# Padding the tiles that TensorE reads to different places modulo 128 bytes in a Mamba2 and Q4 feed-forward kernel

## The chip, the core and the metric

The kernel is one program on one core of a Trainium2 chip. The time is device microseconds from the start to the end of that core's execution. Lower is better. The host only lays data out before the launch.

## What is computed

The input `x` is `(2, 512, 512)`. It is layer-normalised, and two branches read the result: a Mamba2 mixer `s` and a feed-forward net `g` with 4-bit weights. The output is `x + s * silu(g)`.

```python
xn = _layernorm(x)
# mixer: 128 heads of 64, state size 128, 8 groups, chunks of 128 tokens
proj = xn @ in_proj_w.T                       # gate 8192 | x 8192, B 1024, C 1024 | dt 128
xBC  = silu(conv4(xBC) + conv_b)              # depthwise, 4 taps
y    = ssd(x, B, C, D, dt, dt_bias)           # chunked selective scan
yg   = y * silu(gate)
out  = (yg / rms over each group of 1024) * norm_w
s    = out @ out_proj_w.T                     # 8192 -> 512
# feed-forward: Q4_0 weights, hidden size 1376
h    = silu(xn @ W1.T) * (xn @ W3.T)
g    = h @ W2.T
result = x + s * silu(g)
```

## The kernel before

Everything in SBUF is float32. A matrix product with full precision is made of three passes: every operand is split into a high part (rounded to float32r, names ending in `_hi`) and a low part (the rest, `_lo`), and `split_mm` (lines 132 to 138) issues for each of four slices of the contraction, `KT = 4`, the three products high by high (L135), high by low (L136, L137). In `pe.matmul(dst, a, b)` the first operand `a` is the **stationary** one: 128x128, loaded by a weight load (LDWEIGHTS, rows of PEld). The second, `b`, is the **moving** one: it streams 512 columns through the array. The views print `bank<-moving,stationary`.

```python
    for i, (a_hi, a_lo, b_hi, b_lo) in enumerate(terms):
        pe.matmul(dst, a_hi, b_hi, start=(i == 0), stop=False)
        pe.matmul(dst, a_hi, b_lo, start=False, stop=False)
        mm = pe.matmul(dst, a_lo, b_hi, start=False, stop=(i == len(terms) - 1))
```

The mixer goes over 16 bodies (8 groups of heads by 2 sequences) with 8 steps each, 128 steps in all, written out without a loop, by `over_bodies`. The order on every engine is written out by hand, and the steps are software-pipelined: the projections of later steps stand between the scan's pieces of this one. One step of TensorE (`step` inside `@block.tensor`, line 696) is, for nearly all of them:

- `y_off`: 3 float32 matmuls (6 records) with `state` stationary and `c_t` moving, L543;
- `conv`: 12 matmuls 128x512 with `conv_hi`/`conv_lo` stationary, `xn_hi`/`xn_lo` moving, L135 to L137;
- `y_diag`: 8 float32 matmuls (16 records) with `xdt` stationary and `lm` moving, L585, then 3 (6 records) with `b_tok` stationary and `xw` moving, L543;
- `gate_mm`: 12 matmuls with `gate_hi`/`gate_lo` stationary, `xn` moving, L135 to L137;
- `out_mm`: 12 matmuls with the results `y_hi`/`y_lo` **stationary** and the weights `wout_hi`/`wout_lo` **moving**, L631 to L633;
- `extra` and `turn_x`: the B and C projections (12 matmuls each, once a body), and transposes of `xt` or `b_t`, moving `ident`, L693 and L654.

The weight load of each matmul is a record of its own and runs beside the matmul before it. After the mixer the feed-forward stage runs 528 matmuls of the same form (`up_hi`, `up_lo` stationary, `xn` moving) and 33 products of the down projection for each of 8 token tiles (`h` stationary, `w2` moving, L831; the last tile in two halves). The other engines round, split, mask, activate and combine beside this; ScalarE, VectorE and GpSimd wait for TensorE by semaphores and TensorE for them.

Tiles are allocated by `alloc` (line 165) as a stack: each starts where the last one ended, a size is taken up to whole 32 bytes per partition, and a closed scope gives its space to the next. The first tile starts at byte 16512 of each partition. `ctx` holds for the whole kernel, `main` for the mixer, `pre` for the setup, and the feed-forward tiles lie over `main`. All matrices have rows of 512 bytes or more, so that a tile's place modulo 128 is also the place of all its slices. `sh` with its 32 bytes puts everything from `xn_hi` to the end of `cw_all` at 32 modulo 128; `cw_all` (1600 bytes) moves what follows to 96.

Of the kernel before, what the change touches and what calls it, by code (L numbers as in the profile page):

```python
# [22 lines left out]
R32 = mybir.dt.float32r  # L23
I32 = mybir.dt.int32

P = 128
SEQS, SEQ, DIM = 2, 512, 512
KT = DIM // P
HEADS, HD = 128, 64
GROUPS, CHUNK = 8, 128  # L30
INTER = HEADS * HD
GCH = INTER // GROUPS
HALF = GCH // 2
GH = HEADS // GROUPS
NC = SEQ // CHUNK
TT = SEQS * SEQ // P
CONVS = GCH // P + 2
TILES = GCH // P
# [10 lines left out]
SH = 4  # L49
# [101 lines left out]
def build(nc, x, w_conv, w_gate, w_out, w_dt, conv_p, norm_p, head_p, consts, w1q, w1s, w3q, w3s,  # L151
# [9 lines left out]
    with ExitStack() as ctx:  # L161
# [3 lines left out]
        def alloc(stack, name, shape, dt=F32):  # L165
            return stack.enter_context(nc.sbuf_tensor(name, [P] + shape, dt))


        ident = alloc(ctx, "ident", [P])
        mask = alloc(ctx, "mask", [P])  # L170
        sh = alloc(ctx, "sh", [2, SH], I32)
        xn_hi = alloc(ctx, "xn_hi", [KT, SEQS * SEQ], R32)
        xn_lo = alloc(ctx, "xn_lo", [KT, SEQS * SEQ], R32)

        main = ExitStack()

        conv_hi = [alloc(main, f"conv_hi{i}", [KT, P], R32) for i in range(3)]
        conv_lo = [alloc(main, f"conv_lo{i}", [KT, P], R32) for i in range(3)]
        raw_x = alloc(main, "raw_x", [2, DIM])
        raw_b = alloc(main, "raw_b", [DIM])  # L180
        raw_g = alloc(main, "raw_g", [DIM])
        raw_o = alloc(main, "raw_o", [DIM])
        z = alloc(main, "z", [3, SEQ])
        b_t = alloc(main, "b_t", [SEQ])
        cw_all = alloc(main, "cw_all", [GROUPS, CONVS, 5])
        gate_hi = [alloc(main, f"gate_hi{h}", [KT, HALF], R32) for h in range(2)]
        gate_lo = [alloc(main, f"gate_lo{h}", [KT, HALF], R32) for h in range(2)]
        c_t = alloc(main, "c_t", [2, SEQ])
        nw_all = alloc(main, "nw_all", [GROUPS, TILES])
        dc_all = alloc(main, "dc_all", [GROUPS, TILES])  # L190
        xt = alloc(main, "xt", [4, SEQ])
        gm = alloc(main, "gm", [NC, CHUNK])
        b_tok = alloc(main, "b_tok", [NC, P])
        gate = alloc(main, "gate", [4, SEQ])
        lm = [alloc(main, f"lm{i}", [2 * NC, CHUNK]) for i in range(3)]
        hp = [alloc(main, f"hp{h}", [NQ, TILES, 2 * NC]) for h in range(2)]
        rstd = alloc(main, "rstd", [NC])
        rstd_sum = alloc(main, "rstd_sum", [NC])
        neg_half = alloc(main, "neg_half", [8])
        one = alloc(main, "one", [1])  # L200

        pre = ExitStack()


        x_in = alloc(pre, "x_in", [TT, DIM])
        stage = alloc(pre, "stage", [NQ, GROUPS, TILES, 2 * NC])
        wdt_raw = alloc(pre, "wdt_raw", [KT, P])
        wdt_hi = alloc(pre, "wdt_hi", [KT, P], R32)
# [1 line left out]
        ecs = alloc(pre, "ecs", [TT, CHUNK])  # L210
        soft = alloc(pre, "soft", [TT, CHUNK])
        wdt_lo = alloc(pre, "wdt_lo", [KT, P], R32)
        heads = alloc(pre, "heads", [3])
        d_row = alloc(pre, "d_row", [P])
        pick = alloc(pre, "pick", [2, P // 2])
# [6 lines left out]
        wout_hi, wout_lo = [], []  # L222
        for h in range(2):
            wout_hi.append(alloc(main, f"wout_hi{h}", [4, DIM], R32))
            wout_lo.append(alloc(main, f"wout_lo{h}", [4, DIM], R32))
            if h == 0:
                acc = alloc(main, "acc", [TT, DIM])
        sq = alloc(main, "sq", [SEQ])
        sq_sum = alloc(main, "sq_sum", [SEQ])
        y_hi = alloc(main, "y_hi", [2, SEQ], R32)  # L230
        y_lo = alloc(main, "y_lo", [2, SEQ], R32)
        yt = alloc(main, "yt", [2, SEQ])
        ec = [alloc(main, f"ec{i}", [(NC - 1) * CHUNK]) for i in range(2)]
# [1483 lines left out]
```

How the kernel before makes its waits and increments, by code:

```python
def wait(eng, sem, count):  # L84
    if isinstance(count, int) and count <= 0:
        return
    eng.wait_ge(sem, count)
# [253 lines left out]
        def token_steps(eng, b):  # L342
            eng.wait_ge(pa, (N_SOFT + N_EXPS) * b + N_SOFT)
            eng.wait_ge(pd, N_PD * b + 1)
            eng.tensor_tensor(qt[Q_DT][:, half[b], :], qt[Q_DT][:, half[b], :], ecs[:, half[b], :],
                              ALU.add).then_inc(dt_done, 1)
            eng.wait_ge(dt_done, 3 * b + 1)
            eng.tensor_scalar(qt[Q_DT][:, half[b], :], qt[Q_DT][:, half[b], :], DT_MIN, DT_MAX, ALU.max,
                              ALU.min).then_inc(dt_done, 1)
            eng.wait_ge(dt_done, 3 * b + 2)
            eng.tensor_scalar(qt[Q_CD][:, half[b], :], qt[Q_DT][:, half[b], :], heads[:, 2:3], None,
                              ALU.mult).then_inc(dt_done, 1)
# [10 lines left out]
        def wait_gate_piece(eng, group, pos):  # L364
            if group == 0 and pos < 4:
                eng.wait_ge(gate0_in[pos], 16)
            else:
                eng.wait_ge(rawg_in, 16 * (8 * group + pos - 3))
# [9 lines left out]
        def wait_hp(eng, body):  # L378
            if body.n == 0:
                eng.wait_ge(hp0_ev, NQ)
            else:
                eng.wait_ge(hp_in[body.seq], 16 * (body.group + body.seq))
# [1 line left out]
        def store_out(sp, t):  # L385
            sp.wait_ge(r2_done, t + 1)
            h = col_parts(t)[0]
            sp.dma_start(out_t[t][:, h], fh[:, t % 2, h]).then_inc(o_out[t % 2], 16)
```

## Time and profile before

| | before |
|---|---|
| median of 3 runs | 1791.61 us |
| lowest, highest | 1790.51, 1792.0 us |
| span of the profiled execution, first to last instruction | 1789.9 us |
| TensorE busy (PE) | 1775.3 us, 99% |
| weight loads (PEld) | 1462.1 us, 82% |
| VectorE (DVE) | 1427.3 us, 80% |
| GpSimd (POOL) | 1262.4 us, 71% |
| ScalarE (ACT) | 1228.8 us, 69% |

The profiled execution has no time of its own beside its span; the median of the runs is 1.7 us above this span, which is what lies before the first and behind the last instruction. Busy time of a group of matmuls is the union of its records. A record lasts longer than the distance to the next one's start, because matmuls are pipelined, so a group's count times its mean is more than its busy time. A mean duration of one is therefore read against another's, and the cost of a matmul is the distance between two starts in the timeline.

### The profile page before, as it was taken

Reading aid. Unit: us, or ns where it says so; the run is one execution under the profiler, and the core shown is the slowest. Engines: PE = TensorE matmul, PEld = TensorE weight load, DVE = VectorE, ACT = ScalarE, POOL = GpSimd, SP = SyncE. Lnnn points to the kernel's source line nnn. Section 1 sums busy time; section 2 is a strip of 40 time slices with the busy share of each in tenths; the row PEclk is TensorE's granted clock in tenths of the full one; section 3 lists DMA queues with packets and bytes.
Section 4 is the critical chain, followed back from the end, with each engine's and each line's share of the span. In section 5 each row is a group of like instructions: output and inputs, shape, how many; then the busy total and the mean of one; then the engine's idle time right before and its main releaser. Section 6 shows DMA issues by size and latency. Waiting matters only on the chain.

```text
span 1789.9 us, 30329 instructions
## 1 busy us (share of the span) xinstructions
PE 1775.3 (99%) x10357; PEld 1462.1 (82%) x10357; DVE 1427.3 (80%) x2196; ACT 1228.8 (69%) x2456; POOL 1262.4 (71%) x877
## 2 busy tenths in 40 slices
PE   8999999999999999999999999999999999999999
PEld 7788888888888888888888888888888888888877
DVE  7978878878788788788787887887887888878941
ACT  6986777777776777677866777677777677643320
POOL 5677787777777687677776786777776777676630
PEclk9999999999999999999999999999999999999999
DMA  5433333233333242333333342333333333235522
GB/s 200 160 123 101 99 130 107 93 121 107 117 107 110 96 134 94 102 110 116 119 104 95 118 122 96 115 98 117 115 96 111 107 123 101 77 108 162 151 78 94
DMA packets 122595, 202.84 MB, mean 113 GB/s; under 512 B 23056, under 2 KB 60560, under 8 KB 122192
## 3 DMA queue, kind: packets, MB, share of 16 engines
q1 hardware_dynamic: 120720, 197.32, 34.9%
q10 hardware_dynamic: 1728, 3.65, 0.5%
q8 instruction: 82, 1.34, 0.3%
q14 instruction: 65, 0.53, 0.1%
HBM read 193.57 MB, written 7.34 MB: 112 GB/s over the span
## 4 chain that ended last, share of the span: by engine, by line
PE 95%; DVE 3%; POOL 1%; issue 1%; DMA 1%; SPq 0%; ACT 0%; POOLq 0%; DVEq 0%; ACTq 0%
PE bank L137 16%; PE bank L135 16%; PE bank L136 16%; PE bank L543 11%; PE bank L585 7%; PE bank L631 7%; PE bank L633 6%; PE bank L632 6%; PE bank L831 3%; PE bank L693 3%; PE bank L674 1%; DVE z L1189 0%; PE bank L654 0%; DMA q_s<-w1s_dram 0%; DVE x_in L1341 0%
## 5 line engine op out<-in xcount | busy, mean ns | idle before, releaser
L1518 POOL TENSOR_TENSOR yt<-yt,ec 128x384 f32<-128x384 f32 x128 | 174.8, 1366 | 329.7 <-DVE ec L1253 329.7
L1189 DVE SCALAR_TENSOR_TENSOR z<-bank,cw_all,z 128x511 f32<-128x511 f32 (+2 forms) x477 | 356.3, 747 | 11.7 <-ACT z L944 0.5
L905 ACT ACTIVATE lm<-lm,hp 128x128 f32<-128x128 f32 x1024 | 313.2, 390 | 0.8
L1244 DVE TENSOR_TENSOR xdt<-bank,hp 128x512 f32<-128x512 f32 x128 | 88.3, 690 | 222.3 <-PE bank L693 221.0
L135 PE MATMUL bank<-xn_hi,conv_hi 128*128 128x512 f32 x640 | 261.7, 409 | 3.5 <-DVE z L1189 3.4
L1223 DVE SCALAR_TENSOR_TENSOR lm<-lm,gm 128x1024 f32<-128x1024 f32 x128 | 261.2, 2040 | 3.4 <-ACT lm L905 3.4
L137 PE MATMUL bank<-xn_hi,conv_lo 128*128 128x512 f32 x640 | 251.7, 393 | 0.0
L136 PE MATMUL bank<-xn_lo,conv_hi 128*128 128x512 f32 x640 | 250.5, 391 | 0.0
L1522 POOL TENSOR_TENSOR yt<-yt,gate 128x512 f32<-128x512 f32 x128 | 226.7, 1771 | 19.0 <-POOL yt L1518 0.9
L1527 POOL TENSOR_TENSOR conv_lo<-raw_x,conv_hi 128x512 fp32r<-128x512 f32 x124 | 218.4, 1762 | 9.9 <-ACT conv_hi L844 9.8
L944 ACT ACTIVATE z<-bank,cw_all 128x512 f32<-128x512 f32 x128 | 99.1, 774 | 166.5 <-PE bank L137 166.5
L135 PE MATMUL bank<-xn_hi,gate_hi 128*128 128x512 f32 x512 | 212.3, 415 | 0.0
L631 PE MATMUL bank<-wout_hi,y_hi 128*128 128x512 f32 x512 | 202.6, 396 | 0.0
L137 PE MATMUL bank<-xn_hi,gate_lo 128*128 128x512 f32 x512 | 202.0, 395 | 0.0
L136 PE MATMUL bank<-xn_lo,gate_hi 128*128 128x512 f32 x512 | 201.8, 394 | 0.0
L633 PE MATMUL bank<-wout_hi,y_lo 128*128 128x512 f32 x512 | 200.6, 392 | 0.0
L632 PE MATMUL bank<-wout_lo,y_hi 128*128 128x512 f32 x512 | 199.2, 389 | 0.0
L1210 DVE SCALAR_TENSOR_TENSOR lm<-hp,lm 128x1024 f32<-128x1024 f32 x128 | 194.5, 1520 | 0.0
L1504 POOL TENSOR_TENSOR y_lo<-yt,y_hi 128x512 fp32r<-128x512 f32 x128 | 182.3, 1424 | 3.0 <-ACT y_hi L976 3.0
L1554 POOL TENSOR_TENSOR sq_sum<-sq_sum,sq 128x512 f32<-128x512 f32 x111 | 145.1, 1307 | 21.2 <-ACT sq L984 21.2
L585 PEld LDWEIGHTS bank<-lm,xdt 128*64 128x64 f32 x2048 | 109.2, 136 | 45.9 <-issue 44.6
L137 PEld LDWEIGHTS bank<-xn_hi,conv_lo 128*128 128x128 f32 x640 | 120.4, 188 | 26.7
(145 smaller groups left out, 3950.9 us busy)
## 6 DMA issues: line engine op xcount, KB each, us to landing
lm<-cs_d SPq DMA_DIRECT2D x128, 512.0 KB, 4.0
raw_x<-w_conv_dram SPq DMA_DIRECT2D x128, 256.0 KB, 3.1
ec<-e_d SPq DMA_DIRECT2D x256, 96.0 KB, 3.6
raw_o<-w_out_dram SPq DMA_DIRECT2D x64, 256.0 KB, 2.7
raw_g<-w_gate_dram SPq DMA_DIRECT2D x61, 256.0 KB, 2.7
raw_b<-w_conv_dram SPq DMA_DIRECT2D x32, 256.0 KB, 3.4
q_raw<-w1q_dram SPq DMA_DIRECT2D x10, 256.0 KB, 3.8
q_s<-w1s_dram SPq DMA_DIRECT2D x10, 256.0 KB, 4.1
```

What stands on the lines that cost most here:

```text
L135: pe.matmul(dst, a_hi, b_hi, start=(i == 0), stop=False)
L136: pe.matmul(dst, a_hi, b_lo, start=False, stop=False)
L137: mm = pe.matmul(dst, a_lo, b_hi, start=False, stop=(i == len(terms) - 1))
L585: mm = pe.matmul(ps_y[HD * j:HD * j + HD, c * P:(c + 1) * P], xdt[:, c * P + HD * j:c * P + HD * j + HD], lm[n % 3][:, NC * j + c, :], sta ...
L631: pe.matmul(ps_o[c][:, :], y_hi[:, ko % 2, o], w[0], start=first, stop=False)
L632: pe.matmul(ps_o[c][:, :], y_hi[:, ko % 2, o], w[1], start=False, stop=False)
L633: mm = pe.matmul(ps_o[c][:, :], y_lo[:, ko % 2, o], w[0], start=False, stop=last)
L905: e = act.activation(lm[m % 3][:, u, :], lm[m % 3][:, u, :], ACT.Exp, bias=hp[bd.seq][:, Q_CS, k1, u:u + 1])
L1189: dve.scalar_tensor_tensor(dst[:, d:SEQ], src[:, 0:SEQ - d], cw_all[:, bd.group, pos, 3 - d:4 - d], dst[:, d:SEQ], ALU.mult, ALU.add).then ...
L1223: dve.scalar_tensor_tensor(lm_c, lm_c, 1.0, gm[:, :, :].rearrange("p c l -> p (c l)").unsqueeze(1) .broadcast_to((P, 2, SEQ)), ALU.mult, A ...
L1522: pool.tensor_tensor(yt[:, kp % 2, :], yt[:, kp % 2, :], gate[:, kp % 4, :], ALU.mult).then_inc(yg_done, 1)
L1527: pool.tensor_tensor(conv_lo[kx % 2][:, :, :], raw_x[:, kx % 2, :].rearrange("p (k j) -> p k j", k=KT), conv_hi[kx % 2][:, :, :].bitcast(F ...
```

## The change

The change adds small tiles that nobody reads or writes (`shift(name)`, 32 bytes; two of 160 bytes) and allocates the small tiles (`sh`, `rstd`, `rstd_sum`, `neg_half`, `one`, `nw_all`, `dc_all`, `cw_all`) first. No instruction is added, removed or moved on any engine: the programs of before and after differ in line numbers and in addresses alone.

```diff
+        sh = alloc(ctx, "sh", [2, SH], I32)
...
+        cw_all = alloc(ctx, "cw_all", [GROUPS, CONVS, 5])
+        alloc(ctx, "to_line", [40])
         ident = alloc(ctx, "ident", [P])
         mask = alloc(ctx, "mask", [P])
-        sh = alloc(ctx, "sh", [2, SH], I32)
         xn_hi = alloc(ctx, "xn_hi", [KT, SEQS * SEQ], R32)
...
-        conv_hi = [alloc(main, f"conv_hi{i}", [KT, P], R32) for i in range(3)]
-        conv_lo = [alloc(main, f"conv_lo{i}", [KT, P], R32) for i in range(3)]
+        def shift(name):
+            alloc(main, name, [8])
+
+        conv_hi, conv_lo = [], []
+        for i in range(3):
+            if i == 1:
+                shift("sh_ch")
+            conv_hi.append(alloc(main, f"conv_hi{i}", [KT, P], R32))
+        for i in range(3):
+            if i < 2:
+                shift(f"sh_cl{i}")
+            conv_lo.append(alloc(main, f"conv_lo{i}", [KT, P], R32))
...
-        gate_hi = [alloc(main, f"gate_hi{h}", [KT, HALF], R32) for h in range(2)]
-        gate_lo = [alloc(main, f"gate_lo{h}", [KT, HALF], R32) for h in range(2)]
+        gate_hi, gate_lo = [], []
+        for h in range(2):
+            shift(f"sh_gh{h}")
+            gate_hi.append(alloc(main, f"gate_hi{h}", [KT, HALF], R32))
+        for h in range(2):
+            shift(f"sh_gl{h}")
+            gate_lo.append(alloc(main, f"gate_lo{h}", [KT, HALF], R32))
+        shift("sh_c")
         c_t = alloc(main, "c_t", [2, SEQ])
...
             wout_hi.append(alloc(main, f"wout_hi{h}", [4, DIM], R32))
+            shift(f"sh_o{h}")
             wout_lo.append(alloc(main, f"wout_lo{h}", [4, DIM], R32))
+            shift(f"sh_p{h}")
...
         y_hi = alloc(main, "y_hi", [2, SEQ], R32)
+        shift("sh_y")
         y_lo = alloc(main, "y_lo", [2, SEQ], R32)
```

The places that come of it, in bytes modulo 128, from adding up the sizes:

| tiles | before | after |
|---|---|---|
| `xn_hi`, `xn_lo` | 32 | 0 |
| `conv_hi` 0, 1, 2 | 32 | 0, 32, 32 |
| `conv_lo` 0, 1, 2 | 32 | 64, 96, 96 |
| `gate_hi` 0, 1 and `gate_lo` 0, 1 | 96 | 0, 32 and 64, 96 |
| `wout_hi` 0, 1 and `wout_lo` 0, 1 | 96 | 0, 64 and 32, 96 |
| `y_hi`, `y_lo` | 96 | 0, 32 |
| `lm`, `c_t`, `b_tok`, `xt` | 96 | 0 |
| `xdt`, `xw`, `state` | 96 | 32 |
| `b_t` | 32 | 96 |
| `ident` | 0 | 0 |
| `up_hi`, `up_lo`, `w2_hi`, `w2_lo`, `h_hi`, `h_lo` | 32 | 0 |

## Rows read from the trace of the kernel before

**Rows 1.** The page: engines' busy time, then the chain that ended last
```profile
PE 1775.3 (99%) x10357; PEld 1462.1 (82%) x10357; DVE 1427.3 (80%) x2196; ACT 1228.8 (69%) x2456; POOL 1262.4 (71%) x877
...
PE 95%; DVE 3%; POOL 1%; issue 1%; DMA 1%; SPq 0%; ACT 0%; POOLq 0%; DVEq 0%; ACTq 0%
PE bank L137 16%; PE bank L135 16%; PE bank L136 16%; PE bank L543 11%; PE bank L585 7%; PE bank L631 7%; PE bank L633 6%; PE bank L632 6%; PE bank L831 3%; PE bank L693 3%; PE bank L674 1%; DVE z L1189 0%; PE bank L654 0%; DMA q_s<-w1s_dram 0%; DVE x_in L1341 0%
```
**Rows 2.** Cores' span and granted clock; then windows: us, busy (records) by engine, clock, DMA
```profile
core 0: 1789.9 us, clock 0.999
...
60.00:1600.00 1540.00, 1537.62 (x9233) 1265.45 (x9232) 1262.00 (x1967) 1135.43 (x2290) 1151.22 (x782) 1.00 0.35 111
```
**Rows 3.** Timeline of PE, conv projection: start us, duration us, operation
```profile
502.81 0.39 PE L136 MATMUL bank<-xn_lo,conv_hi 128*128 128x512 f32 x1
...
505.11 0.39 PE L137 MATMUL bank<-xn_hi,conv_lo 128*128 128x512 f32 x1
```
**Rows 4.** The same timeline, gate projection
```profile
507.45 0.39 PE L136 MATMUL bank<-xn_lo,gate_hi 128*128 128x512 f32 x1
...
509.79 0.40 PE L137 MATMUL bank<-xn_hi,gate_lo 128*128 128x512 f32 x1
```
**Rows 5.** The same timeline, output projection, right behind the gate projection
```profile
510.02 0.40 PE L631 MATMUL bank<-wout_hi,y_hi 128*128 128x512 f32 x1
510.26 0.39 PE L632 MATMUL bank<-wout_lo,y_hi 128*128 128x512 f32 x1
...
512.55 0.39 PE L633 MATMUL bank<-wout_hi,y_lo 128*128 128x512 f32 x1
```
**Rows 6.** The same timeline, feed-forward stage
```profile
1649.90 0.39 PE L137 MATMUL bank<-xn_hi,up_lo 128*128 128x512 f32 x1
...
1652.85 0.39 PE L135 MATMUL bank<-xn_hi,up_hi 128*128 128x512 f32 x1
```
**Rows 7.** Groups by line and form, 512-wide matmuls: busy us, mean ns | idle before
```profile
L137 PE MATMUL bank<-xn_hi,conv_lo 128*128 128x512 f32 x640 | 251.7, 393 | 0.0
L136 PE MATMUL bank<-xn_lo,conv_hi 128*128 128x512 f32 x640 | 250.5, 391 | 0.0
...
L631 PE MATMUL bank<-wout_hi,y_hi 128*128 128x512 f32 x512 | 202.6, 396 | 0.0
L137 PE MATMUL bank<-xn_hi,gate_lo 128*128 128x512 f32 x512 | 202.0, 395 | 0.0
L136 PE MATMUL bank<-xn_lo,gate_hi 128*128 128x512 f32 x512 | 201.8, 394 | 0.0
L633 PE MATMUL bank<-wout_hi,y_lo 128*128 128x512 f32 x512 | 200.6, 392 | 0.0
L632 PE MATMUL bank<-wout_lo,y_hi 128*128 128x512 f32 x512 | 199.2, 389 | 0.0
...
L136 PE MATMUL bank<-xn_lo,up_hi 128*128 128x512 f32 x160 | 62.3, 389 | 0.0
...
L831 PE MATMUL bank<-w_lo,h_hi 128*128 128x512 f32 x70 | 27.2, 389 | 0.0
```
**Rows 8.** The same view, short matmuls of the scan
```profile
L585 PE MATMUL bank<-lm,xdt 128*64 128x128 f32 x2048 | 140.1, 279 | 0.9 <-DVE ec L1253 0.9
...
L543 PE MATMUL bank<-c_t,state 128*128 128x128 f32 x768 | 107.9, 277 | 0.0
L693 PE MATMUL bank<-ident,xt 128*128 128x128 f32 x512 | 76.7, 272 | 0.5 <-DVE state L1309 0.5
...
L543 PE MATMUL bank<-c_t,b_t 128*128 128x128 f32 x128 | 16.8, 274 | 0.0
...
L654 PE MATMUL bank<-ident,b_t 128*128 128x128 f32 x64 | 9.6, 272 | 0.0
```
**Rows 9.** The same view, weight loads
```profile
L136 PEld LDWEIGHTS bank<-xn_lo,gate_hi 128*128 128x128 f32 x512 | 96.4, 188 | 17.8
...
L136 PEld LDWEIGHTS bank<-xn_lo,up_hi 128*128 128x128 f32 x160 | 30.1, 188 | 6.2
```

More of the change, by code:

```diff
@@ L166, in alloc @@
             return stack.enter_context(nc.sbuf_tensor(name, [P] + shape, dt))
+        sh = alloc(ctx, "sh", [2, SH], I32)
+        rstd = alloc(ctx, "rstd", [NC])
+        rstd_sum = alloc(ctx, "rstd_sum", [NC])
+        neg_half = alloc(ctx, "neg_half", [8])
+        one = alloc(ctx, "one", [1])
+        nw_all = alloc(ctx, "nw_all", [GROUPS, TILES])
+        dc_all = alloc(ctx, "dc_all", [GROUPS, TILES])
+        cw_all = alloc(ctx, "cw_all", [GROUPS, CONVS, 5])
+        alloc(ctx, "to_line", [40])
         ident = alloc(ctx, "ident", [P])
         mask = alloc(ctx, "mask", [P])
-        sh = alloc(ctx, "sh", [2, SH], I32)
         xn_hi = alloc(ctx, "xn_hi", [KT, SEQS * SEQ], R32)
@@ L184, in build @@
         b_t = alloc(main, "b_t", [SEQ])
-        cw_all = alloc(main, "cw_all", [GROUPS, CONVS, 5])
-        gate_hi = [alloc(main, f"gate_hi{h}", [KT, HALF], R32) for h in range(2)]
-        gate_lo = [alloc(main, f"gate_lo{h}", [KT, HALF], R32) for h in range(2)]
+        gate_hi, gate_lo = [], []
[6 more added lines that the diff above has]
+        shift("sh_c")
         c_t = alloc(main, "c_t", [2, SEQ])
-        nw_all = alloc(main, "nw_all", [GROUPS, TILES])
-        dc_all = alloc(main, "dc_all", [GROUPS, TILES])
         xt = alloc(main, "xt", [4, SEQ])
@@ L196, in build @@
         hp = [alloc(main, f"hp{h}", [NQ, TILES, 2 * NC]) for h in range(2)]
[L197 to L200, printed above, removed]
         pre = ExitStack()
         x_in = alloc(pre, "x_in", [TT, DIM])
+        alloc(pre, "sh_st", [8])
         stage = alloc(pre, "stage", [NQ, GROUPS, TILES, 2 * NC])
@@ L212, in build @@
         wdt_lo = alloc(pre, "wdt_lo", [KT, P], R32)
+        alloc(pre, "sh_h", [40])
         heads = alloc(pre, "heads", [3])
```

## The prediction

> **What bounds the kernel now.** I read the busy times and the chain first, then the clock and a long window, then the timeline, then the groups by form. The page says that PE is busy for 99% of the span and holds 95% of the chain that ended last, with DVE at 80% and POOL at 71% [rows 1]. The window from 60 to 1600 us holds 1537.62 us of busy PE in 1540.00, at granted clock 1.00, so 2.4 GHz [rows 2]. TensorE hardly ever waits for another engine, nor does its clock leave room. What the kernel takes is the sum of the distances between matmul starts. L135 to L137 and L631 to L633 together are 67% of the chain [rows 1], and all of them are 128x512 matmuls, so their distance is the quantity to look at.
>
> That distance is not one number. The gate projection goes from 507.45 to 509.79 in 10 steps: 234 ns [rows 4]. The feed-forward projection, the same instruction on the same moving tiles, goes from 1649.90 to 1652.85 in 13 steps: 227 ns [rows 6]. The conv projection needs 2.30 us for 10 steps, 230 ns [rows 3], and the output projection 2.53 us for 11 steps, 230 ns, of which its first is 240 ns (510.02 to 510.26) [rows 5]. The weight loads beside them last the same 188 ns in the gate and in the feed-forward group [rows 9], and nothing waits. The mean durations say the same over the whole run: feed-forward 389, gate 394 and 395, conv 391 and 393, output 396, 389 and 392 [rows 7]. A duration is about 161 ns above the distance (389 against 227, 394 against 234), so a difference of two mean durations can be used as a difference of two distances. I do that below.
>
> What differs between gate and feed-forward, as far as the code shows, is the place of the stationary tile: 96 against 32, with `xn` moving at 32. I call the stationary place minus the moving place, modulo 128, the **relation**. It is 64 for gate and 0 for feed-forward, conv, output and down projection. Relation 64 looks 5 to 6 ns dearer than relation 0 at its best. But conv and output also have relation 0 and yet average 392: the output group starts with a slow one right after the gate group and its three lines differ (396, 389, 392) though their tiles all lie at 96 [rows 7]. So a group in relation 0 pays after a switch, and only then comes down to 389. This settling costs about 3 ns a matmul averaged over a group of 12.
>
> **The change, part by part.** No instruction changes on any engine or queue; only addresses do. The relations become:
>
> | family (512-wide matmuls) | relation before | after |
> |---|---|---|
> | conv (1920) | 0 | 0 with high and 64 with low weights in buffer 0; 32 and 96 in buffers 1 and 2 |
> | gate (1536) | 64 | 0 and 64 in half 0, 32 and 96 in half 1 |
> | output (1536) | 0 | 0, 96, 32 in half 0 (L631, L632, L633); 64, 32, 96 in half 1 |
> | feed-forward up (528) and down (297, a few narrower) | 0 | 0 |
>
> 1. **The 4992 matmuls of the first three rows.** Relations 32 and 96 stand in no 512-wide row, so their cost is bounded. From below: the fastest steady level in the trace, 389. From above: 397, which is the 396 of L631 [rows 7] with a nanosecond on it, the line with the 240 ns start. In relation 0 and 64 I know the steady levels, 389 and 394, but after the change no family has one relation: within every group of three the weights' place goes high, high, low, by 64 bytes and back. That is the state right after a switch, for good. The nearest rows for a mixed state are conv and output, both 392. I take 392.5 for all three families, a little above since none of them can come to rest. Conv: 392 to 392.5, 1920 x 0.5 ns = +1.0 us. Gate: 394.5 to 392.5, 1536 x 2.0 ns = -3.1 us. Output: mean of 396, 389 and 392 is 392.3, so 1536 x 0.2 ns = +0.3 us. Sum -1.8 us.
> 2. **Feed-forward.** Relation 0 stays, only the absolute place goes from 32 to 0. Output and feed-forward both reach 389 with tiles at 96 and at 32 [rows 7], so the absolute place counts for nothing: 0 us.
> 3. **Short matmuls of the scan.** `c_t` with `state` (relation 0) 277, `c_t` with `b_t` (relation 64) 274, `ident` with `xt` (relation 96) and with `b_t` (relation 32) both 272 [rows 8]. They don't follow the relation: 0 us. The two of L543 differ by 3 ns, with 1536 records of `state` and `xw` that is at most 4.6 us either way, and I keep a third of it in the range. `lm` with `xdt`, 279, is bounded by the same.
> 4. **The other engines.** Their tiles move too. PE covers them: DVE has 362 us of the span free, POOL and ACT more than 500 us [rows 1]. If PE became 20 us faster, DVE would still be at 81%; next late would be the scores and `xdt` that L585 waits for (0.9 us of idle time in all now, [rows 8]).
>
> Sum: 1789.9 - 1.8 = 1788.1 us of span, and with the 1.7 us by which the median of 1791.6 stands above this span, **1789.8 us**, 0.1% under the median.
>
> One rule of the Trainium skill speaks against any effect. The rows first: with equal loads beside them (188 ns [rows 9]) gate takes 234 ns and feed-forward 227 a matmul [rows 4, 6]. The page "TensorE: Matmul & The Clock Gate", Part 2, says that the moving operand and the weight load have independent read ports, so that the loading doesn't take bandwidth from the running matmul, and gives 215.7 ns for a 512-wide one back to back. By that figure, which no row here comes near, each of the 4992 could still lose about 11 ns below the feed-forward level, 56 us in all; I take nothing of it into the sum.
>
> **The rivals.** About 0.2% (3.6 us) is what a measurement of this kernel can tell from no change.
>
> - *A, washed out (my forecast), 0.42.* All families in the mixed state. The level of 392.5 may be 391 or 394: that gives -(1.9+5.4+2.0) = -9.3 us, or +(3.8-0.8+2.6) = +5.6 us. For it: the two families now in transition both average 392 although one is preceded by short matmuls and the other by gate. Of the 0.42 I count 0.22 as the same, 0.13 as faster, 0.07 as slower.
> - *B, the spread removes the collisions, 0.30.* If weight load and moving stream collide when they hit the same place, different places for neighbours keep them apart, and all 4992 come to the feed-forward level or below: conv 1920 x 3 = 5.8, gate 1536 x 5.5 = 8.4, output 1536 x 3.3 = 5.1 us, together -19.3 us, 1772.3 us. For it: gate is over 5 ns from what the array can do in the same shape. Against it: the best level of the trace belongs to tiles that all lie at one place.
> - *C, the settled relation 0 is lost, 0.22.* The other side. The mechanism is the place of the second weights in each group of three: relation 64 costs what gate costs, and 32 and 96 no less. Conv then goes from 392 to 394.5 (+4.8 us), output from 392.3 to 394.5 (+3.4 us), gate stays: +8.2 us, 1799.8 us. If each step costs what the first line of the output group does, 397, it is 9.6 + 3.8 + 7.2 = +20.6 us, 1812 us. A common level of all three above 392.9, their weighted mean now, is a loss, and above 393.6 one of over 3.6 us. For it: relation 0 is left by most of conv and by all of output but L631 in half 0, and gained by a part of gate alone.
> - *D, nothing happens, 0.06.* TensorE's two reads don't meet at all, and the families differ by something that the change doesn't touch, say what the other engines do beside them. Then every term is nil: 1791.6 us. For it: gate and feed-forward lie in different stages with different work beside them. Against it: the gate level holds for 10 steps to the nanosecond. By the page "SBUF — State Buffer", section "Who interferes with whom", this would be the outcome, since it says that TensorE never waits for anyone there; the two levels of [rows 4, 6] are not explained by this rule.
>
> **How the numbers follow.** Faster: 0.13 of A and 0.30 of B, 0.43. The same: 0.22 of A and 0.06 of D, 0.28. Slower: 0.07 of A and 0.22 of C, 0.29. The time is A's, 1789.8 us. A alone reaches from 1782 to 1797. Both signs carry weight, so the range takes in B's centre with 4 us beyond it and C to the point where the level is about 395: 1768 to 1803 us. What is left out is B far below the feed-forward level (0.1) and C at the level of 396 and over (0.08).
>
> **What would show it.** Right for A: conv, gate and output all within 391 to 394 in the groups by form, gate lower by 1 to 3 and conv not lower; feed-forward at 389 still; short matmuls within 1 ns; in the timeline no stretch of equal distances in gate. B is right if gate and conv come to 389 or less and the timeline shows equal distances of 227 or below. C is right if conv rises to 394 or more. D is right if gate stays at 394 with 234 ns steps. The prediction is wrong in its base if the feed-forward level moves, since then the absolute place counts, or if PE's waits for DVE grow beyond a few us, since then PE is not the whole account.

## The result: 0.27% slower

| | before | after |
|---|---|---|
| median | 1791.4 us (7 runs, 1790.51 to 1792.0) | 1796.19 us (7 runs, 1795.69 to 1796.66) |
| span of the profiled execution | 1789.9 us | 1793.9 us |

The ratio is 1.0027 with a 95% interval of 1.0018 to 1.0037. The change costs 4.8 us. That lies inside the forecast range of 1768 to 1803 us, but on the other side of no change than the forecast time of 1789.8.

The profile after, to be read against [rows 1, 2]: busy times, chain by engine, clock, and the long window. The lines of the changed kernel stand 22 lines further down, so L543, L585, L631, L632, L633, L693 and L831 are L565, L607, L653, L654, L655, L715 and L853.

```profile
PE 1778.7 (99%) x10357; PEld 1461.6 (81%) x10357; DVE 1428.8 (80%) x2196; ACT 1228.8 (68%) x2456; POOL 1263.3 (70%) x877
...
PE 96%; DVE 2%; POOL 1%; issue 0%; DMA 0%; SPq 0%; ACT 0%; DVEq 0%; POOLq 0%
```
```profile
core 0: 1793.9 us, clock 1.000
...
60.00:1600.00 1540.00, 1537.72 (x9190) 1262.87 (x9187) 1260.10 (x1961) 1134.64 (x2290) 1146.81 (x779) 1.00 0.35 110
```

Next to nothing waits more than it did: PE is idle for 15.2 us of its span where it was idle for 14.6, at full clock in both, but in the same 1540 us it gets through 9190 records instead of 9233. The 512-wide matmuls have become a little longer or shorter, as the groups by form show (busy us, mean ns | idle before), against [rows 7]:

```profile
L137 PE MATMUL bank<-xn_hi,conv_lo 128*128 128x512 f32 x640 | 252.4, 394 | 0.0
L136 PE MATMUL bank<-xn_lo,conv_hi 128*128 128x512 f32 x640 | 251.5, 393 | 0.0
...
L137 PE MATMUL bank<-xn_hi,gate_lo 128*128 128x512 f32 x512 | 201.9, 394 | 0.0
L653 PE MATMUL bank<-wout_hi,y_hi 128*128 128x512 f32 x512 | 201.8, 394 | 0.0
L655 PE MATMUL bank<-wout_hi,y_lo 128*128 128x512 f32 x512 | 201.6, 394 | 0.0
L136 PE MATMUL bank<-xn_lo,gate_hi 128*128 128x512 f32 x512 | 201.5, 394 | 0.0
L654 PE MATMUL bank<-wout_lo,y_hi 128*128 128x512 f32 x512 | 201.1, 393 | 0.0
L607 PE MATMUL bank<-lm,xdt 128*64 128x128 f32 x2048 | 140.1, 279 | 0.8 <-DVE ec L1275 0.8
...
L565 PE MATMUL bank<-c_t,state 128*128 128x128 f32 x768 | 107.9, 277 | 0.0
L715 PE MATMUL bank<-ident,xt 128*128 128x128 f32 x512 | 76.7, 272 | 0.5 <-DVE state L1331 0.5
...
L136 PE MATMUL bank<-xn_lo,up_hi 128*128 128x512 f32 x160 | 62.3, 389 | 0.0
```

Conv has risen by one to two nanoseconds. Output's three lines (396, 389 and 392 before) have drawn together at 393 to 394, one and a half higher in the mean. Gate has fallen by at most one, and the feed-forward and the short matmuls are within a nanosecond of where they were.

Mean durations are whole nanoseconds, so I also added up the distances between starts, group by group, for the 153 conv, 125 gate and 121 output groups of twelve that stand complete in both traces. A group goes from its first matmul's start to the start of whatever follows. These totals are the measure used in all that follows:

| us in all groups | conv | gate | output | sum |
|---|---|---|---|---|
| before | 443.6 | 360.7 | 334.0 | 1138.3 |
| after | 447.8 | 359.5 | 335.9 | 1143.2 |
| difference | +4.2 | -1.2 | +1.9 | +4.9 |

The three families account for the loss, which is 4.8 us between the medians and 4.0 us between the spans of the two profiled executions. With the groups that hold a wait or stand at the start and the end, all records of the three families together differ by 4.3 us.

The distances themselves, median over all groups of a kind, in ns, show how. In each group the first and the last number hold the entry from and the exit to another kind of matmul.

```
before
conv behind state    314 231 236 228 232 231 227 227 227 227 227 318   sum 2924
gate                 315 233 233 233 233 233 233 233 233 233 233 232   sum 2880
output behind gate   240 227 231 236 228 233 231 227 227 227 227 231   sum 2762
after
conv behind state    314 232 233 231 231 232 230 228 235 232 234 320   sum 2952
gate                 315 232 236 233 232 231 232 231 231 232 231 231   sum 2868
output behind gate   232 230 232 232 230 231 232 230 232 232 230 230   sum 2772
```

Before, the groups come to rest: output and most of conv at 227, gate at 233. After, conv, output and half 0 of gate do not; only half 1 of gate comes to 231 to 232, at its seventh step. The medians of after are taken over buffers and halves with different patterns. To within a nanosecond the same series (231 236 228 232 231, then 227) stands before in 86 of the 124 conv groups behind the short matmuls and, one step later, in 121 of the 122 output groups behind gate, whatever else runs at the time. Nearly all the other groups enter the same series earlier or later, so that the 30 conv groups behind output reach 227 only at their eleventh step. The unevenness is not noise of other engines.

### The profile page after: what moved, and what is told of

It is laid out like the page before. It is cut to its first block, busy times and chain, and to the rows that moved or that the text cites. A ratio compares the mean times of both kernels' runs of the same rounds, so it can differ in the third digit from the quotient of the medians.

```text
span 1793.9 us, 30329 instructions
## 1 busy us (share of the span) xinstructions
PE 1778.7 (99%) x10357; PEld 1461.6 (81%) x10357; DVE 1428.8 (80%) x2196; ACT 1228.8 (68%) x2456; POOL 1263.3 (70%) x877
## 4 chain that ended last, share of the span: by engine, by line
PE 96%; DVE 2%; POOL 1%; issue 0%; DMA 0%; SPq 0%; ACT 0%; DVEq 0%; POOLq 0%
PE bank L135 17%; PE bank L137 17%; PE bank L136 17%; PE bank L565 12%; PE bank L607 7%; PE bank L653 7%; PE bank L655 7%; PE bank L654 7%; PE bank L853 3%; PE bank L715 3%; PE bank L696 1%; PE bank L676 0%; DVE z L1211 0%; DVE x_in L1363 0%; DMA x_in<-x_dram 0%
## 5 line engine op out<-in xcount | busy, mean ns | idle before, releaser
L653 PE MATMUL bank<-wout_hi,y_hi 128*128 128x512 f32 x512 | 201.8, 394 | 0.0
L655 PE MATMUL bank<-wout_hi,y_lo 128*128 128x512 f32 x512 | 201.6, 394 | 0.0
L654 PE MATMUL bank<-wout_lo,y_hi 128*128 128x512 f32 x512 | 201.1, 393 | 0.0
L607 PEld LDWEIGHTS bank<-lm,xdt 128*64 128x64 f32 x2048 | 109.2, 136 | 47.0 <-issue 45.7
```

The source lines that it names most:

```text
L607: mm = pe.matmul(ps_y[HD * j:HD * j + HD, c * P:(c + 1) * P], xdt[:, c * P + HD * j:c * P + HD * j + HD], lm[n % 3][:, NC * j + c, :], sta ...
L653: pe.matmul(ps_o[c][:, :], y_hi[:, ko % 2, o], w[0], start=first, stop=False)
L654: pe.matmul(ps_o[c][:, :], y_hi[:, ko % 2, o], w[1], start=False, stop=False)
L655: mm = pe.matmul(ps_o[c][:, :], y_lo[:, ko % 2, o], w[0], start=False, stop=last)
```

## The experiments

Two theories were put to the test. **Theory 1, relation**: a matmul costs what its two places make it cost, whatever came before. **Theory 2, settling**: a stream of matmuls with unchanging places comes to rest at a level that its relation sets, and every change of place costs some uneven steps. A step is the distance from one matmul's start to the next one's. From here on places and relations are counted modulo 256 bytes, for a reason that the experiments show. The first kernel is the changed one without its pads, and the diffs of the others are against this first; all leave the instructions as they are and differ in pads alone. A pad behind the moved tiles puts the tiles that follow back to place 0, and the setup tiles are padded along where they lie over moved ones. Where no number of runs is given, the time is that of a single execution. Beside them the kernel before took 1791.29 us (one_place, gate_plus64, gate_32_96, conv_low128), 1790.87 (the three spreads and wout_plus64), 1791.38 (state32, btok32, both32) and 1790.38 (gate_plus128). `shift` takes the pad's bytes as its second argument.

### All at one place

```diff
-            if i == 1:
-                shift("sh_ch")
...
-            shift(f"sh_gh{h}")
...
-            shift(f"sh_o{h}")
...
-        shift("sh_y")
```

> All pads taken out, the small tiles still first: every tile that TensorE reads, of all families, lies at place 0 modulo 256. Theory 1 (cost by relation alone): each 512-wide matmul costs what the places of the weights and of the moving tile make it cost, whatever came before. Relation 0 costs what conv and output cost before, 392, so gate gains 2.5 ns x 1536 and nothing else moves: -3.8 us, 1787.6. Theory 2 (settling): a stream of matmuls whose places don't change settles at equal distances of 227 ns in relation 0 (mean duration 389), and the dearer ones are the first after another place or another kind of matmul. Then gate's 12 come from 2880 ns to 2811 to 2833 (-6 to -9 us over 128), output's from 2762 to 2720 (-5.4 us), conv's behind output from 2766 to 2720 (-1.4 us): 1775 to 1779 us, gate at 389 to 391 and the output lines all at 389.

Measured: 1780.42 us (5 runs, 1779.74 to 1781.0), ratio to before 0.9939 with an interval of 0.9926 to 0.9953. It beats both kernels: 10.9 us under before, 15.8 us under the change. The groups by form of this kernel:

```profile
L137 PE MATMUL bank<-xn_hi,conv_lo 128*128 128x512 f32 x640 | 250.3, 391 | 0.0
L136 PE MATMUL bank<-xn_lo,conv_hi 128*128 128x512 f32 x640 | 249.9, 391 | 0.0
...
L642 PE MATMUL bank<-wout_hi,y_hi 128*128 128x512 f32 x512 | 199.7, 390 | 0.0
L644 PE MATMUL bank<-wout_hi,y_lo 128*128 128x512 f32 x512 | 199.5, 390 | 0.0
L643 PE MATMUL bank<-wout_lo,y_hi 128*128 128x512 f32 x512 | 199.2, 389 | 0.0
```

Its timeline of an output group, behind gate (start us, duration us):

```profile
506.00 0.39 PE L137 MATMUL bank<-xn_hi,gate_lo 128*128 128x512 f32 x1
506.23 0.39 PE L642 MATMUL bank<-wout_hi,y_hi 128*128 128x512 f32 x1
506.45 0.39 PE L643 MATMUL bank<-wout_lo,y_hi 128*128 128x512 f32 x1
...
508.72 0.39 PE L644 MATMUL bank<-wout_hi,y_lo 128*128 128x512 f32 x1
```

From 506.23 to 508.72 are 11 steps of 226 ns, and the first is as short as the last; before, it took 240 ns [rows 5]. Output's relation was 0 before too. What has gone is the switch from gate's place to its own, and with it the 39 ns a group (median 2762 to 2723). By theory 1 output would not have moved. Totals: conv 442.1 (-1.5), gate 356.5 (-4.2), output 329.4 us (-4.6). Theory 1's 1787.6 is out. Theory 2's 1775 to 1779 is missed by a microsecond or two, in gate: I had expected 2811 to 2833 ns a group there, and it takes 2847, since its first ten steps are uneven.

```
conv behind state    314 231 236 228 232 231 227 227 227 227 227 318   sum 2924
gate                 312 229 233 236 224 231 236 228 232 231 227 227   sum 2847
output behind gate   227 227 227 227 227 227 227 227 227 227 227 230   sum 2723
```

### One family moved as a whole

```diff
+            shift(f"sh_gh{h}", (64, 0)[h])
             gate_hi.append(alloc(main, f"gate_hi{h}", [KT, HALF], R32))
...
+        shift("sh_c", 192)
         c_t = alloc(main, "c_t", [2, SEQ])
```

> As one_place, but the four gate tiles 64 bytes further: relation 64 for gate, 0 for all others. Both theories: gate's distances are 233 to 234 ns (duration 394). They differ at the switch: theory 1 leaves output at its level of one_place; theory 2 wants a slow first output matmul of 240 ns and a few uneven ones behind it, some 40 ns a group of 12, and so about 5 us on output and 9 us on gate over one_place.

Measured: 1789.54 us. Gate settles at 233 again from its third step (total 361.7, +5.2 us), and output behind it reads 236 224 231 236 228 232 231, then 227: total 333.2, +3.8 us, although every tile of output has the place that it has in one_place. Its timeline (start us, duration us):

```profile
509.44 0.40 PE L644 MATMUL bank<-wout_hi,y_hi 128*128 128x512 f32 x1
509.68 0.39 PE L645 MATMUL bank<-wout_lo,y_hi 128*128 128x512 f32 x1
...
511.97 0.39 PE L646 MATMUL bank<-wout_hi,y_lo 128*128 128x512 f32 x1
```

That is 2.53 us for the 11 steps that take 2.49 us in one_place, a little less than the 40 ns a group and 5 us that I had expected. This is the settling as its own measurement, and together with gate's own level it takes away 9.1 of the 10.9 us that one_place had won.

```diff
+            shift(f"sh_o{h}", (64, 0)[h])
             wout_hi.append(alloc(main, f"wout_hi{h}", [4, DIM], R32))
...
+        shift("sh_y", 192)
         y_hi = alloc(main, "y_hi", [2, SEQ], R32)
```

> one_place with the four wout tiles, which are the moving ones, 64 bytes further; y, the stationary ones, stay at 0. What settles is either the place of the loaded weights or the pair. If the weights' place alone sets the rhythm, output has equal distances from its first step, at the level of its relation (227 if the relation counted only in one direction, 233 as gate otherwise), +0 to +9 us. If a new moving place upsets it too, the first five or six steps are uneven as after the switch from gate to output before, and the rest equal.

Measured: 1789.69 us. Here the *moving* tiles are moved and the loaded ones stay. The relation is 64 again modulo 128, but counted modulo 256 it is 192, since now the moving side lies further. Output doesn't rest in equal steps; from its fourth on it repeats 232 226 229: total 334.7, +5.3 us, and conv, which comes next, has more uneven steps (+3.0 us). So the pair counts, not the weights' place alone, and of my two cases neither was right: it does not settle in equal distances but in a repeating set of three.

```diff
+            shift(f"sh_gh{h}", (128, 0)[h])
             gate_hi.append(alloc(main, f"gate_hi{h}", [KT, HALF], R32))
...
+        shift("sh_c", 128)
```

> one_place with the four gate tiles 128 bytes further. If relation and settling go by the place modulo 128, this is one_place to the nanosecond: gate total 2847 ns, output 2723, 1780.4 us. If the period is 256 bytes, gate has the level of a relation of its own, and output pays for the switch: gate 2840 to 2890, output 2730 to 2765, 1782 to 1790 us.

Measured: 1786.34 us. Gate is uneven throughout (total 359.2, +2.7 us), output pays 3.8 us for the switch. 128 bytes are not neutral, so the period of this behaviour is not 128 bytes. That 256 bytes are neutral stands in conv_low128 below: its two pads of 128 put the gate tiles 256 bytes further against `xn` than in one_place, and a gate group takes 2848 ns against 2847.

```diff
         for h in range(2):
+            shift(f"sh_g{h}", (32, 64)[h])
             gate_hi.append(alloc(main, f"gate_hi{h}", [KT, HALF], R32))
-        for h in range(2):
             gate_lo.append(alloc(main, f"gate_lo{h}", [KT, HALF], R32))
+        shift("sh_c", 160)
```

> As one_place, but gate's half 0 (high and low) 32 bytes further and half 1 (high and low) 96 bytes further, so that relations 32 and 96 are seen unmixed. If only the unrest of changing places was the cost of the spread, each half has equal distances, at a level of 227 to 234 ns. If relations 32 and 96 are dear in themselves, a half lies above 234. If they are free of collisions, a half lies below 227, down to 216 to 220.

Measured: 1787.66 us. Half 0, all at relation 32, goes 232, 235, 232, 235 in turn; half 1, all at relation 96, between 229 and 238. A group takes 2876 and 2888 ns, against 2847. Gate's total is +4.4 us, output's +2.6 us. None of the three cases of the expectation came: the steps are not equal, and their means are 233 and 234 ns, no more than the level of relation 64. So relations 32 and 96, unmixed, are as dear as 64. Of the relations tried by themselves (32, 64, 96, 128, and 192 in wout_plus64) none is better than 0; 160 and 224, which the change also uses, were not tried by themselves.

### High and low weights apart, and one family of the change alone

```diff
+            shift(f"sh_cl{i}", (128, 0, 0)[i])
             conv_lo.append(alloc(main, f"conv_lo{i}", [KT, P], R32))
+        shift("sh_x", 128)
         raw_x = alloc(main, "raw_x", [2, DIM])
```

> As one_place, but the three low conv tiles 128 bytes further. If places count modulo 128, nothing changes: conv as in one_place, 389 once settled, equal distances of 227. If they count modulo 256 or more, conv is as uneven as with the spread, mean 392 to 396, some +3 to +8 us.

Measured: 1786.88 us, conv total 448.4, +6.3 us, with conv at 395 in the groups by form of this kernel:

```profile
L137 PE MATMUL bank<-xn_hi,conv_lo 128*128 128x512 f32 x640 | 253.1, 395 | 0.0
L136 PE MATMUL bank<-xn_lo,conv_hi 128*128 128x512 f32 x640 | 252.9, 395 | 0.0
```

All conv tiles have the same place modulo 128 here. Behind output, which leaves it settled, a conv group now repeats 227 232 234, a step for each of the three products of `split_mm`, whose weights are high, high and low in turn. That is 231 ns in the mean. Relation 0 by itself takes 227 and relation 128 by itself 232 (the mean of gate's steps in gate_plus128), which for two high and one low would make 229. So going to and fro between two places costs something beside the two levels.

Then the pads of the change come back for one family at a time: conv_spread (below), gate_spread and out_spread.

```diff
+            shift(f"sh_ch{i}", (0, 32, 0)[i])
             conv_hi.append(alloc(main, f"conv_hi{i}", [KT, P], R32))
...
+            shift(f"sh_cl{i}", (32, 32, 0)[i])
             conv_lo.append(alloc(main, f"conv_lo{i}", [KT, P], R32))
+        shift("sh_x", 160)
```

> one_place with the conv tiles alone at the places of the change (high 0, 32, 32, low 64, 96, 96). If the loss of the change is a sum of losses within families, conv's groups take 447 to 448 ms-thousandths, that is 447.8 us in total as in the changed kernel, +5.7 us over one_place, gate and output stay at 356.5 and 329.4 us: 1786 us. If the unrest is carried from one family into the next, gate or output rise too.

(The "ms-thousandths" of this expectation are microseconds.)

```diff
+            shift(f"sh_gh{h}", (128, 32)[h])
             gate_hi.append(alloc(main, f"gate_hi{h}", [KT, HALF], R32))
...
+            shift(f"sh_gl{h}")
             gate_lo.append(alloc(main, f"gate_lo{h}", [KT, HALF], R32))
+        shift("sh_c")
```

> one_place with the gate tiles alone at the places of the change (128, 160 high, 192, 224 low, modulo 256). Gate's groups in total 359.5 us as in the changed kernel, +3.0 us over one_place; and output, which follows gate, gets a few uneven steps at the switch of the weights' place, +1 to +4 us. 1784 to 1788 us. If a switch costs nothing, output stays at 329.4 us and the time is 1783.5.

```diff
+            shift(f"sh_o{h}")
             wout_lo.append(alloc(main, f"wout_lo{h}", [4, DIM], R32))
+            shift(f"sh_p{h}")
...
+        shift("sh_y")
         y_lo = alloc(main, "y_lo", [2, SEQ], R32)
...
+        shift("sh_e", 96)
         ec = [alloc(main, f"ec{i}", [(NC - 1) * CHUNK]) for i in range(2)]
```

> one_place with wout and y alone at the places of the change. Output's groups in total 335.9 us as in the changed kernel, +6.5 us over one_place: 1787 us, and +1 us where conv follows output. If it were the absolute place or the relation of the high weights only, less than 3 us.

Measured, against one_place, one execution each:

| us | time | conv | gate | output |
|---|---|---|---|---|
| one_place | 1780.42 | 442.1 | 356.5 | 329.4 |
| conv_spread | 1785.73 | **447.9** | 355.5 | 329.9 |
| gate_spread | 1786.32 | 442.1 | **360.7** | 331.4 |
| out_spread | 1790.14 | 443.4 | 357.2 | **337.0** |
| after, all three | 1796.19 | 447.8 | 359.5 | 335.9 |

Each family loses by its own spread: 5.3, 5.9 and 9.7 us in time. Conv's total is that of the changed kernel, as expected. Gate lost 4.2 us instead of 3.0, output 7.6 instead of 6.5, and out_spread missed its forecast of 1787 us by 3 us. The three come to 20.9 us, all together to 15.8. The totals show how they overlap: alone, gate_spread also costs output 2.0 us, and out_spread costs conv 1.3 and gate 0.7 us, while in the changed kernel these families are uneven anyway. That one more switch then costs less is my reading of it. One family gained: in conv_spread gate takes 1.0 us less than in one_place, though its tiles have the same place, because 76 of its 125 groups have six uneven steps instead of ten. How conv ends is carried through the short matmuls into gate. Per matmul, output loses most, 7.6 us over 1536 or 4.9 ns, against 3.0 ns in conv and 2.7 ns in gate. Output is the family in which both the moving and the loaded tiles are spread; that this is why was not tried by itself.

### Who sets the entry

state32 has the second of these pads, btok32 the first with its return, both32 all of them.

```diff
+        shift("sh_b", 32)
         gm = alloc(main, "gm", [NC, CHUNK])
         b_tok = alloc(main, "b_tok", [NC, P])
+        shift("sh_t", 224)
...
+        shift("sh_d", 32)
         xdt = alloc(main, "xdt", [NC * P])
```

> one_place with xdt, xw and state, which serve the short matmuls of the scan, 32 bytes further; all tiles of the 512-wide matmuls stay at 0. What is asked is who sets the uneven steps at the entry of conv (five, 22 ns a group over settled) and gate (ten, 37 ns a group) behind the short matmuls. If the places of the short ones' tiles set the phase in which a group is entered, the pattern behind them changes: conv's or gate's group total moves by 10 to 40 ns, the time by 1 to 6 us to either side of 1780.4. If the phase comes from somewhere else, both totals stay (2922 and 2847 ns) and the time is 1780.

> one_place with gm and b_tok, which is loaded as weights by the short matmuls just ahead of gate, 32 bytes further. If the place of the last weights loaded ahead of a group sets its entry, gate's total moves from 2847 by 10 to 40 ns and conv's stays at 2922: 1775 to 1785 us. If not, 1780.

> Both moves together. If each sets the entry of its own family only, conv's total is that of state32 and gate's that of the closer of the two; if the moving and the loaded tile of the short matmuls count as a pair, gate's entry is again that of one_place, since xw and b_tok have relation 0 again.

Measured: state32 1779.55 us (4 runs, 1779.23 to 1779.7), btok32 1780.21 (1779.81 to 1780.74), both32 1779.51 (1779.34 to 1779.7). In state32 a conv group behind the short matmuls reads 314 232 231, then 227: three uneven steps fewer, 2909 ns instead of 2924. Gate is unchanged at 2847 in all three. So `state` (or `xw`, `xdt`, which moved with it) sets part of conv's entry, and `b_tok`, the tile loaded last ahead of gate, doesn't set gate's; both32 adds nothing to state32. The gain of under 1 us beside one_place can't be told apart by the ratios to before, 0.9935 (0.9918 to 0.9951) and 0.9939 (0.9926 to 0.9953); the shorter conv groups show it. What sets gate's ten uneven steps stays open, but for conv_spread, where gate's entry changed with the places of the conv tiles.

## Why the prediction was wrong

- **What bounds the kernel: right.** PE stayed at 99%, its idle time grew by 0.6 us, and the loss is in the distances of the three families.
- **Feed-forward, short matmuls, other engines at nothing: right.** 389 to 390 for feed-forward, and 279, 277, 272 for the short ones, within a nanosecond of [rows 7, 8]. The absolute place of the feed-forward tiles, 32 to 0, does nothing.
- **The settling after a switch: right, and stronger than I used it.** I read it from the 396, 389 and 392 of the output lines [rows 7]; gate_plus64 shows it alone, 3.8 us on a family none of whose tiles moved.
- **The step that failed is the level of the mixed state**, "I take 392.5 for all three families". It measured about 393.5 for conv, 394 for gate and 393.7 for output. By term: conv +1.0 forecast, +4.2 measured; gate -3.1 and -1.2; output +0.3 and +1.9. A nanosecond and a bit on 4992 matmuls is the whole error and turns -1.8 into +4.9. The row I leaned on was the wrong kind of row: conv and output at 392 were not in a mixed state, they were in transition for half of each group and at rest for the other half, and the resting half, at 389, had pulled the mean down. The uneven half alone averages 231 to 232 ns, that is about 393. The timeline of the trace before had it: [rows 3] cover the uneven and the resting steps in one difference of 2.30 us, and I averaged over both instead of splitting them. Splitting alone would not have given the result: at 393 for all three the sum is +1.9 - 2.3 + 1.1 = +0.7 us. The other half to one nanosecond is what the changed relations cost beyond a switch, and no row before had it; gate_32_96 shows relations 32 and 96 at 233 and 234 ns, and conv_low128 the price of going to and fro.
- **Counting modulo 128 was wrong too.** gate_plus128 and conv_low128 show that a relation of 128 is not 0. The table's 0 and 64 for gate's half 0 are really 128 and 192, and the 0 of output's L631 is 128: the change leaves no gate or output matmul at relation 0. My sum took one level for all mixed states, so this didn't enter it; it did enter the argument for rival C, which counts relation 0 as gained by a part of gate.
- **The signs that I named could not tell A from C.** Conv at 393 and 394, output at 393 and 394, gate lower by one in one of its lines: nearly all signs of A hold (only the rest of gate's half 1 at 231 to 232 speaks against it), and half of C's (conv at 394 or more) as well, while the time went the other way than A's.
- **My rival C was the nearer one**: "the settled relation 0 is lost". Its mechanism, the place of the second weights, is part of it; the level of relations 32 and 96, 233 to 234 ns when nothing is mixed (gate_32_96), is as it supposed, no less than gate's. Its price for one common level of 394.5, +8.2 us, was too high, since the mean came to lie between. I had given it 0.22 against 0.42 for the washed-out case, whose own slow edge of +5.6 us holds the result.
- **Rival B is refuted**: different places don't make the matmuls faster. Eight kernels with some tiles of the 512-wide matmuls moved all took 5 us or more longer than the one with none moved.
- **Rival D is refuted.** Pads alone moved the time by 15.8 us between the change and one_place, with the same instructions on all engines. The Trainium skill's page "TensorE: Matmul & The Clock Gate", Part 2, says that weight loading takes no read bandwidth from the running matmul. The runs don't show the ports themselves, but if that rule is read as a cost free of places, the traces disagree: 227 ns at relation 0 and 233 at 64, with the same loads beside them. No run here came near the 215.7 ns of that page: the best steady level of all kernels is 227. The Trainium skill's page "SBUF — State Buffer", section "Who interferes with whom", says that TensorE never waits for anyone at SBUF. As a rule about other engines no run here contradicts it; what the pads changed is how TensorE's own two operands lie to each other.

That a better kernel lay in the opposite direction could have been read from the trace before: 389 stood in the rows of the one stage in which every tile has one place and nothing is switched.

## What to carry to other kernels

When TensorE is full, look at the distance between matmul starts, and compare the same form of matmul in different stages; here 227 and 234 ns in one kernel pointed the way to 10.9 us. Put all stationary and moving tiles of consecutive matmul groups at one place modulo 256 bytes; here it cost one reordering of small tiles and one pad. And when a mean of a group lies between two levels, look whether it is a level or a mixture in time before using it as a price.

## What the runs showed of the hardware

- The spacing of back-to-back 512-wide float32r matmuls with a weight load beside each depends on byte places: 227 ns settled at relation 0 (one_place), 233 at relation 64 (gate_plus64), 232 and 235 in turn at relation 32, uneven at 96 (gate_32_96) and at 128 (gate_plus128), and 232 226 229 in turn at 192 (wout_plus64). The extremes of single steps inside the groups of all kernels are 224 and 241 ns. Why a place costs what it does, no run shows.
- The period is 256 bytes and not 128: moving only the low conv tiles by 128 cost 6.3 us in conv (conv_low128), moving gate by 128 cost 2.7 us in gate and 3.8 us in output (gate_plus128), while gate tiles moved by 256 against `xn` cost 1 ns a group (2848 against 2847, conv_low128).
- The uneven steps on the way to relation 0 are a fixed series that leads back into rest, entered at different points: 229 233 236 224 231 236 228 232 231 227. It stands in full in conv behind output before and in gate in one_place, and its end in conv behind the short matmuls and in output.
- Settled stretches keep a common beat of 6.67 ns, 16 cycles at the granted 2.4 GHz. Taking the starts in the trace's nanoseconds modulo this beat, and taking out an even drift of 1.5 ns a millisecond, the settled stretches of a family (four equal steps or more) fall on one point, to within 0.6 cycles, through the whole span of the kernel before: 106 of conv, 127 of output, 123 of gate. Gate, 64 bytes above conv, lies 4 cycles later; output, 64 bytes below, 4 cycles earlier; in gate_plus64 gate again lies 4 cycles behind conv; and in one_place conv and output (154 and 123 stretches) fall together. 64 bytes for a quarter of the beat would make 256 bytes for all of it, which fits with the period above. That the memory serves TensorE's two reads in such a turn is my reading of it and was not tested by itself.
